# The low part of the gated rows on VectorE instead of GpSimd, and ScalarE's cast of them ahead of its casts of the down weights

## The reference

```python
        logits = jnp.einsum('th,eh->te', x, gate_w)
        scores = jax.nn.softmax(logits, axis=-1)
        topk_w, topk_idx = jax.lax.top_k(scores, K)
        combine = jnp.sum(jax.nn.one_hot(topk_idx, E, dtype=x.dtype) * topk_w[..., None], axis=1)
        gu = jnp.einsum('th,ehj->etj', x, w_gate_up)
        h = _swiglu(gu, I)
        y = jnp.einsum('eti,eih,te->th', h, w_down, combine)
        gu_s = x @ shared_gate_up
        y = y + _swiglu(gu_s, SI) @ shared_down
```

## Time and profile before

| | us |
|---|---|
| median of 3 runs | 2095.75 |
| lowest and highest of them | 2095.16, 2096.2 |
| the profiled execution's own time | 2098.51 |
| its span, from the first to the last instruction | 2096.7 |

### The profile page before, as it was taken

How to read it: one execution, slowest core, us unless ns; L and a number is a source line. 1 busy time by engine, 2 the same in 40 slices (tenths; PEclk the granted TensorE clock), 3 DMA queues, 4 the chain that set the end, 5 groups by cost and what they waited for, 6 DMA issues and landing times. The chain is left out here.

```text
span 2096.7 us, 35409 instructions
## 1 busy us (share of the span) xinstructions
PE 1678.1 (80%) x13401; PEld 864.9 (41%) x13401; DVE 1463.9 (70%) x2115; ACT 997.4 (48%) x1549; POOL 571.1 (27%) x568
## 2 busy tenths in 40 slices
PE   0579999777999858888984977974696888888697
PEld 0353333344333223444441543543463555555364
DVE  3558998446898478999963364364624999999667
ACT  4345777434677713333333222222133777777532
POOL 0250000252000033344321122123261444444255
PEclk9889999998999989999996988996798999999899
DMA  8000000000000000000002000002004665345234
GB/s 298 1 2 2 2 2 2 1 1 1 2 2 2 2 1 1 1 0 0 1 1 91 1 1 1 1 1 96 32 2 144 195 195 153 113 154 183 94 102 139
DMA packets 49393, 105.96 MB, mean 51 GB/s; under 512 B 7096, under 2 KB 10392, under 8 KB 48720
## 3 DMA queue, kind: packets, MB, share of 16 engines
q1 hardware_dynamic: 37632, 75.99, 10.4%
q0 software_dynamic: 7424, 21.00, 3.9%
q10 hardware_dynamic: 4176, 6.82, 0.9%
HBM read 149.68 MB, written 21.01 MB: 81 GB/s over the span
## 5 line engine op out<-in xcount | busy, mean ns | idle before, releaser
L624 ACT ACTIVATE attn_prob<-attn_ps_t 128x512 f32<-128x512 f32 x576 | 312.6, 595 | 127.9 <-PE attn_ps_t L591 126.3
L643 DVE TENSOR_REDUCE attn_mx<-attn_ps_s 128x2 f32<-128x1024 f32 (+3 forms) x304 | 342.8, 1163 | 41.5 <-PE attn_ps_s L572 38.0
L136 PE MATMUL sparse_ps_g<-sparse_wg,sparse_xT 128*128 128x352 f16 x1152 | 190.5, 316 | 54.7 <-DVE sparse_xT L1900 54.7
L604 PE MATMUL attn_ps_o<-attn_prob,V 128*32 128x256 f32 x2304 | 174.8, 389 | 3.6 <-ACT attn_prob L624 2.7
L1905 DVE SCALAR_TENSOR_TENSOR sparse_wg<-sparse_raw_g,sparse_wg 128x2816 f16<-128x2816 f32 x48 | 148.4, 3092 | 37.9 <-ACT sparse_wg L1857 37.8
L136 PEld LDWEIGHTS sparse_ps_g<-sparse_wg,sparse_xT 128*128 128x128 f16 x1152 | 107.8, 99 | 128.8 <-DVE sparse_xT L1900 77.7
L778 POOL TENSOR_TENSOR wo_o<-O,wo_o 128x512 f16<-128x512 f32 (+1 forms) x16 | 18.4, 1153 | 496.0 <-ACT wo_o L750 495.9
L1942 POOL TENSOR_TENSOR sparse_h<-sparse_hid,sparse_h 128x352 f16<-128x352 f32 x48 | 87.7, 1826 | 217.4 <-ACT sparse_h L1876 217.4
L1021 PE MATMUL lin_ps_z<-w,lin_xT 128*128 128x512 f16 x576 | 136.2, 387 | 0.0
L1857 ACT ACTIVATE sparse_wg<-sparse_raw_g 128x2816 f16<-128x2816 f32 x48 | 122.0, 2541 | 17.2 <-DMA sparse_raw_g<-in_L_ffn_w_gate_up_dram 17.2
L849 PE MATMUL ffn_ps_fc<-wfcT,ffn_xT 128*128 128x512 f16 x512 | 123.6, 393 | 8.1 <-DVE ffn_xT L926 8.1
(11 more groups left out here) (320 smaller groups left out, 3407.2 us busy)
## 6 DMA issues: line engine op xcount, KB each, us to landing
sparse_raw_g<-in_L_ffn_w_gate_up_dram SPq DMA_DIRECT2D x48, 1408.0 KB
sparse_raw_d<-in_L_ffn_w_down_dram SPq DMA_DIRECT2D x48, 512.0 KB
y_d<-sparse_y SPq DMA_DIRECT2D x48, 256.0 KB, 3.6
sparse_raw_d<-in_L_ffn_w_down_dram SPq DMA_DIRECT2D x48, 192.0 KB
prep_w_fc<-in_L_ffn_w_fc_dram SPq DMA_DIRECT2D x4, 1024.0 KB, 15.6
X<-in_L_attn_x_dram ACTq DMA_DIRECT2D x1, 4096.0 KB, 39.6
prep_w_proj<-in_L_ffn_w_proj_dram SPq DMA_DIRECT2D x4, 1024.0 KB, 22.4
x_d<-route_x SPq DMA_DIRECT2D x16, 256.0 KB, 2.0
```

Source lines behind the costliest of these rows:

```text
L136: last = pe.matmul(out, a(k), b(k), start=(k == 0 and n == 0), stop=(k == chunks - 1 and n == 2))
L604: last = pe.matmul(ps_o[32 * jj:32 * jj + 32, 256 * half:256 * half + 256], V[:, kt, 4 * jg + jj, :], prob[(2 * q + jj // 2) % 4][:, half, ...
L624: act.activation(prob[g % 4][:, par, :, :], ps_t[:, (2 * g + par) % 3, :, :], ACT.Exp, scale=HD ** -0.5).then_inc(exp_done, 1)
L643: dve.tensor_reduce(mx[x % 2][:, c, :, at:at + per], ps_s[:, 2 * (r % 2):2 * (r % 2) + 2, 0:per * n].rearrange("p e (h k) -> p e h k", k=n ...
```

## The change

Three edits, all in `sparse_experts`. `hlo`, the subtraction that makes the low part of the gated rows, moves from GpSimd's list to VectorE's, between `xevac` and `down_lo`; its waits and its semaphore are the same. GpSimd is left with the gathers. In ScalarE's list `hhi` and `down_hi` change places.

```diff
@@ block.scalar @@
-                unrolled(NG, [(1, gate_hi), (2, tanh), (3, hevac), (2, down_hi), (2, hhi), (3, yevac)])
+                unrolled(NG, [(1, gate_hi), (2, tanh), (3, hevac), (2, hhi), (2, down_hi), (3, yevac)])
@@ block.vector @@
+                def hlo(t):
+                    u = t % 2
+                    dve.wait_ge(hh_done, t + 1)
+                    after(dve, ht_done, t - 1)
+                    dve.tensor_tensor(h2[u][:, 1, :], hid[u][:, :], h2[u][:, 0, :], ALU.subtract).then_inc(hl_done, 1)
+
-                unrolled(NG, [(1, gate_lo), (2, swiglu), (1, xevac), (2, down_lo)])
+                unrolled(NG, [(1, gate_lo), (2, swiglu), (1, xevac), (2, hlo), (2, down_lo)])
@@ block.gpsimd @@
-                def hlo(t):
-                    u = t % 2
-                    pool.wait_ge(hh_done, t + 1)
-                    after(pool, ht_done, t - 1)
-                    pool.tensor_tensor(h2[u][:, 1, :], hid[u][:, :], h2[u][:, 0, :], ALU.subtract).then_inc(hl_done, 1)
-
-                unrolled(NG, [(0, gather), (2, hlo)])
+                unrolled(NG, [(0, gather)])
```

## The result

The changed kernel takes **2165.05 us** in the median (2163.28 to 2165.85), the kernel before, on the same chip, 2095.45 (2093.37 to 2096.2): a ratio of 1.0333, 95% interval 1.0315 to 1.0351. The forecast was 2163.8, in a range of 2157 to 2176. The profiled execution has a span of 2163.9 us, 67.2 more than before; 2164.7 was forecast for it.

What follows compares the result with a forecast made beforehand. A ring of VectorE and ScalarE was taken to set the sparse stage's 7.57 us step; 67.6 us for the casts plus 0.4 at the stage's end, on 2095.75, gave 2163.8 us, range 2157 to 2176.

Steps and rivals of the forecast that it cites:

- The ring: Sparse stage: VectorE's L1905, L1911, L1915, then ScalarE's L1876, L1889, L1857, wait for each other and fill the 7.57 us step.
- ScalarE's order, 1.47 us a step: Down casts L1863 and L1864 leave ScalarE's idle time and land between L1876 and L1889, adding 1.47 us a step.
- 46 times, 67.6 us: The casts' cost falls on L1857 of tiles 2 to 47: 46 x 1.47 = 67.6 us, bounds 63.0 and 77.7.
- The sum, 68.0 us: Whole kernel: 67.6 for the casts plus 0.4 at the stage's end, 68.0 us slower.
- VectorE's subtraction, 0.52 and hidden: The moved 128x352 subtraction takes 0.52 us on VectorE and hides in the gap before L1921, costing nothing.
- L1923 from 1.34 to 0.68: VectorE's L1923 runs faster without GpSimd's subtraction beside it, 0.66 us a step, but this buys no time.
- TensorE: Sparse stage: TensorE stays off the critical path, with about 2.4 us free a step in gaps of 0.9 and 1.5.
- End of the stage, +0.4: Last tile: subtraction 0.8 us shorter, down casts holding the last down products up to 1.5 longer; taken as +0.4.
- The gather costs nothing: GpSimd's gather now starts beside L1905, lands 4.2 us later in the median, is wanted over 17 us on: no cost.
- My rival: Gather collides with L1905, holding it 1.24 us a step, 57 us in all, 2221 us; chance 4%.

Runs made afterwards that it cites:

- e1: Kernel before with ScalarE's new order only (hhi ahead of down_hi), subtraction left on GpSimd: 2163.13 us, ratio 1.0324.
- e3: Changed kernel with down_hi cut in two: 128x1024 cast back ahead of the gated rows' cast, 96x512 one behind it: 2120.23 us, ratio 1.0122.
- e7: Changed kernel with ScalarE's old order of casts and the copy of the result, L1889, moved behind L1857 of the next step: 2075.79 us, ratio 0.991.
- e2: Changed kernel with ScalarE's old order back, so only the subtraction moved to VectorE: 2095.26 us, ratio 1.0003.
- e4: Kernel before with ScalarE's cast of the gate-up weights one step earlier, ahead of the cast of the gated rows: 2220.85 us, ratio 1.0601.
- e5: e4's order of ScalarE with the subtraction on VectorE, where the changed kernel has it: 2094.48 us, ratio 0.9998.
- e6: As e5, with the subtraction behind VectorE's down subtractions: 2065.82 us, ratio 0.9855.

## Why the prediction was right

- **The ring**: right. e1, e3, e7 and the change itself lengthen or shorten the step by the pitch put in or taken out.
- **ScalarE's order, 1.47 us a step**: 9.03 - 7.57 = 1.46 measured. The pitch of L1864, which the trace of before didn't show, was taken as 0.53 and is 0.52.
- **46 times, 67.6 us**: 67.1 from the first L1905 to the last.
- **The sum, 68.0 us**: 67.2 between the two profiled executions, 69.6 between the medians, where the interval of the ratio allows 66.0 to 73.5. That 2163.8 was met within 1.3 us is in part luck: the end of the stage came out 1.5 us below its term, and some 1.2 us ahead of the first L1905 and behind the last L1889, for which there was no term, went the other way.
- **VectorE's subtraction, 0.52 and hidden**: it takes 0.53 and ends at 5.17 us of the step; L1921 starts at 6.11 (6.12 forecast), behind 0.94 us of waiting. e2 shows that it is free.
- **L1923 from 1.34 to 0.68**: right, as is that it brings nothing while the ring stands.
- **TensorE**: gaps of 0.88 and 1.50 us against 0.9 and 1.5 told, and a granted clock of 1.00.
- **End of the stage, +0.4**: wrong in sign. From the start of the last L1905 to that of the last L1889 it is 2041.88 - 2026.35 = 15.53 us against 1975.34 - 1958.70 = 16.64 before. This term of the sum failed, by 1.5 us: I had looked at who waits for whom and not at the speed of the last down products. Before and after:

```profile
1971.64 3.67 PE L1845 MATMUL sparse_ps_y<-sparse_wd,sparse_hT 128*128 128x512 f16 x9 [0.96 <-ACT sparse_hT L1883]
```

```profile
2039.74 2.10 PE L1845 MATMUL sparse_ps_y<-sparse_wd,sparse_hT 128*128 128x512 f16 x9 [2.29 <-ACT sparse_hT L1883]
```

The nine took 3.67 us before, at a granted clock of 0.55 (1971.64 to 1975.31), so nearly all of the time at the level of 1.2 GHz, and 2.10 after, at 1.00, the level of 2.4, although the gap ahead of them had grown from 0.96 to 2.29 us. Why the clock had fallen in the one and not in the other is open. Without this difference of 1.57 us the term would have been -1.11 + 1.57 = +0.46, near the 0.4 forecast, so what was missed is the clock and not the balance of the waits.

- **The gather costs nothing**: right for the time, wrong in its duration. L1905 doesn't feel it (3093 ns), but the gather itself takes 3.39 us where I had taken 1.24, and lands 6.2 us after its issue in the median where I had taken 4.2:

```profile
1783.15 3.39 POOL L1941 DMA_INDIRECT sparse_xg<-x_d,token  x1 [5.63 <-PE sparse_ps_x L1810]
```

```profile
DMA to landing us min/median/max: 3.2/6.2/10.2
```

My rival had VectorE held by GpSimd. It is GpSimd that is held, and the gather is wanted two steps of 9.03 us on; TensorE waited for a gather only once, at the start of the stage. The section of the Trainium skill that I had drawn on (SBUF — State Buffer, Who interferes with whom) lets only GpSimd instructions that read SBUF collide with L1905; I had taken the gather for one that doesn't, and the row shows it held. The kernel's gather does take its list of tokens from SBUF; that this is the reason is likely, but no run here shows it.

## What to carry to other kernels

When each of two engines idles a little in every step, look for the ring: write down start to start which instructions of the one and of the other follow each other, and see whether they add up to the step. Work that sits in the idle time ahead of the ring's wait is free, and the same work behind that wait costs its full pitch in each step, though neither engine is busy all the time (here 93 and 79 of 100 us). Opening a ring moves waits to places that had room until then (e4: a GpSimd instruction that came to stand beside a long one of VectorE; e5: a load's place in the queue), so the next bounds are to be read before the first is taken away.

## What the hardware showed

**GpSimd's subtraction and VectorE's hold each other.** GpSimd's 128x352 subtraction takes 0.85 us with VectorE idle (e1), 1.84 when it starts just behind L1921 and 3.54 when it starts just behind L1905 (e4). Each of the held ones ends 0.71 us after VectorE's instruction: before, 1759.09 + 1.84 = 1760.93 against 1759.00 + 1.22 = 1760.22; in e4 1784.76 against 1784.05. So the 1.32 in the earlier trace rows wasn't a free one either: it starts at 1968.80, beside the L1921 below, and ends at 1970.12, again 0.71 us after that one's 1969.41. L1923 in turn, which starts while the subtraction runs, ends 0.54 us after it (1761.47 and 1760.93), and takes 1.34 us instead of 0.68.

```profile
1968.18 1.23 DVE L1921 SCALAR_TENSOR_TENSOR sparse_wd<-sparse_raw_d,sparse_wd 128x1024 f16<-128x1024 f32 x1
```

**The gathers are held too, and L1905 isn't held by one.** In three kernels in which a gather starts at different points of L1905 (its row above for the changed kernel, those of e2, e7 and e6 below), it ends 0.82 us after L1905 does: 1786.54 and 1785.72 in the changed one, 1783.37 and 1782.55 in e2, 1784.72 and 1783.90 in e7. In e6, where it starts 0.07 us behind L1905's end, it takes 0.94. So the 1.24 us of the earlier trace rows, which the prediction took for a gather's own time, was a held one as well: it ends at 1762.32, 0.85 us after L1923 (1761.47). L1905 itself, which starts at 1761.97 while that gather runs, takes its 3.09 us all the same.

```profile
1781.44 1.93 POOL L1941 DMA_INDIRECT sparse_xg<-x_d,token  x1 [5.64 <-PE sparse_ps_x L1810]
```

```profile
1783.27 1.45 POOL L1941 DMA_INDIRECT sparse_xg<-x_d,token  x1 [5.63 <-PE sparse_ps_x L1810]
```

```profile
1782.93 0.94 POOL L1941 DMA_INDIRECT sparse_xg<-x_d,token  x1 [5.81 <-PE sparse_ps_x L1810]
```
